# Scores broadcast by transposes, row sums from the accumulator, both deviations in one chain on POOL

## The chip, the core and the metric

The kernel runs on one core of a Trainium2 chip. The time is device time of one execution in microseconds (us). Before the change three runs took 2421.63, 2421.95 and 2422.08 us; the median is 2421.95.

The engines are called as in the profile: PE multiplies matrices (PEld loads its weights), DVE is the vector engine, ACT the scalar engine, POOL the GpSimd engine, and SP issues the DMAs. Each has its own queue of instructions and runs it in order; semaphores tie the queues together.

## The reference

The input x is 128 graphs of 128 nodes with 256 features, adj 128 matrices of 128 x 128. A graph attention layer and a mixture of eight experts follow one another, each behind a layer norm and with a residual:

```python
def _layernorm(x, axis=-1, eps=1e-5):
    m = jnp.mean(x, axis=axis, keepdims=True)
    v = jnp.var(x, axis=axis, keepdims=True)
    return (x - m) / jnp.sqrt(v + eps)

def _L0_gnn_ref(h, adj, W, a):
    Wh = jnp.einsum('bnd,df->bnf', h, W)
    s1 = Wh @ a1
    s2 = Wh @ a2
    e = s1[:, :, None] + s2[:, None, :]
    e = jnp.where(e > 0, e, ALPHA * e)
    e = e + jnp.log(adj + EPS)
    alpha_w = jax.nn.softmax(e, axis=-1)
    return jnp.einsum('bij,bjf->bif', alpha_w, Wh)

def _L0_ffn_ref(x, ...):
    feat = jnp.mean(x, axis=0)
    w = jax.nn.softmax(feat @ Wr + br, axis=-1)
    h = jnp.einsum('bfd,edh->bfeh', x, W1) + b1
    h = jax.nn.relu(_bn(h, g1, be1, m1, v1))
...
    return jnp.einsum('bfed,fe->bfd', y, w)

x = x + _L0_gnn_ref(_layernorm(x, axis=-1), adj, L0_gnn_W, L0_gnn_a)
x = x + _L0_ffn_ref(_layernorm(x, axis=-1), ...)
```

## The kernel before

The 128 graphs are worked in 32 groups of four. The first block (the graph layer, up to about 285 us) takes one group per step in a software pipeline, written out as `step(g, layer)` for each engine. The second block (the experts) takes 32 tiles of eight experts each and is not touched but for a scale factor. The order of work is the order in which each engine's `step` is written; there is no scheduler. Of the 35 steps, seven at the start and four at the end are written out, 24 run in two hardware loops: `layer == 1` (16 steps, which also prepare the first expert weights in two parts, `wq_hi` on ACT and `wq_lo` on POOL) and `layer == 2` (8 steps, `w_hi` and `w_lo`). In step g the group `a` is g - 1, `b` is g - 2, `t` is g - 3, `h` is g - 4 and `nxt` is g + 1.

In one step of the graph layer:

- PE computes h for group b (`ps_h`, from pT and wh, L750), projects group g (`ps_wide`, L734), transposes x of group nxt (`ps_xT`, L703), transposes p of group a (`ps_pT`, L771), and spreads the scores s2 of group g over a square by a product with the identity (`ps_s`, L778). `ps_xT` and `ps_h` are two views of the same memory `ps_th`, in two halves of 512 columns.
- ACT adds s1 (`s_sb`, L508), scales half of x1 for a running sum (`x1s_high`, L516), takes the exponential (`e_sb`, L528), copies a mean (`mean_all`, L534), scales the projection by 1/deviation into `wh` (L548, two pairs of copies), and copies `xnT` (L561) and `pT` (L568) out of PSUM.
- DVE adds the other half to the running sum `acc` (printed as resb, L621), takes the leaky relu (`l_sb`, L636), the reciprocal of the row sums (`rinv`, L640), aggregates the statistics of x1 (`mv`, L594), takes the row maximum (`neg_m`, L645), adds the residual (`x1`, printed as h or w_bc, L664), multiplies by adj (`p_sb`, L674), takes the statistics of the next x (L580) and of x1 (L588), and sums the rows of p (`rowsum`, L686).
- POOL adds `x1s_high` to acc (L441), turns the variance of x1 into `rstd_all` (L449, L452), does its share of the weights (L459 to L476), and turns the statistics of the next x into `rstd` (L403 to L415), the last by a pow.
- SP loads x two groups ahead, stores x1, loads the residual and adj.

Of the kernel before, what the change touches and what calls it, by code (L numbers as in the profile page):

```python
# [24 lines left out]
P = 128  # L25
# [13 lines left out]
def adj_ffn(nc, x, adj, gnn_w, gnn_a, wr, br, w1, b1, g1, be1, m1, v1, w2, b2, g2, be2, m2, v2, wo, bo, out):  # L39
# [17 lines left out]
    with ExitStack() as ctx:  # L57
# [9 lines left out]
        eps_cols = sb("eps_cols", [P, GB])  # L67
# [11 lines left out]
        rstd_all = sb("rstd_all", [P, G, GB])  # L79
# [22 lines left out]
        rstd2_done = sem("rstd2_done")  # L102
# [82 lines left out]
        with ExitStack() as sa:  # L185
# [16 lines left out]
            st1 = [sba(f"st1_{i}", [P, GB, 6]) for i in range(2)]  # L202
            sum1 = sba("sum1", [P, GB])
            dif1 = sba("dif1", [P, GB])
            var1 = sba("var1", [P, GB])
            sqr1 = sba("sqr1", [P, GB])
            ve1 = sba("ve1", [P, GB])
            mean_w = sba("mean_w", [P, P])
            rstd1 = [sba(f"rstd1_{i}", [P, GB]) for i in range(2)]
# [10 lines left out]
            st2 = sba("st2", [P, GB, 6])  # L220
            mv2 = [sba(f"mv2_{i}", [P, GB, 2]) for i in range(2)]
            ve2 = sba("ve2", [P, GB])
# [31 lines left out]
            rstd1_done = sem("rstd1_done", sa)  # L254
# [18 lines left out]
            rowsum_done = sem("rowsum_done", sa)  # L273
# [4 lines left out]
            stats2_done = sem("stats2_done", sa)  # L278
            ve2_done = sem("ve2_done", sa)
# [44 lines left out]
            def _(sp):  # L324
                def load_x(g):
                    p = g[1]
                    wait(sp, xnT_ready, num(g) - 1)
                    wait(sp, bnst1, num(g) - 1)
                    sp.dma_start(x_sb[p][:, :, :], x_g[num(g)]).then_inc(x_loaded[p], 16)
# [13 lines left out]
                def step(g, layer):  # L343
# [24 lines left out]
                    if exists(g):  # L368
                        wait(sp, p_done, num(g) - 1)
                        sp.dma_start(adj_sb[p][:, :, :], adj_g[num(g)]).then_inc(adj_loaded[p], 16)  # L370
# [14 lines left out]
            def _(pool):  # L385
                nc.gpsimd.memset(ident[:, :], 0.0).then_inc(bn_step, 1)
                nc.gpsimd.memset(minus_half[:, :], -0.5).then_inc(w_done, 2)
                nc.gpsimd.memset(eps_cols[:, :], LN_EPS)
# [9 lines left out]
                def rstd_1(g):  # L398

                    p = g[1]  # L400
                    pool.wait_ge(bnst1, num(g) + 1)
                    wait(pool, rstd1_done, num(g))
                    nc.gpsimd.tensor_tensor(dif1[:, :], st1[p][:, :, 1], st1[p][:, :, 4],  # L403
                                            ALU.subtract).then_inc(var1_step, 1)
                    nc.gpsimd.tensor_tensor(sum1[:, :], st1[p][:, :, 2], st1[p][:, :, 5],
                                            ALU.add).then_inc(var1_step, 1)
                    pool.wait_ge(var1_step, 4 * num(g) + 2)
                    nc.gpsimd.tensor_tensor(sqr1[:, :], dif1[:, :], dif1[:, :], ALU.mult).then_inc(var1_step, 1)
                    nc.gpsimd.tensor_scalar(var1[:, :], sum1[:, :], 4.0 / D, 4.0 * LN_EPS, ALU.mult,
                                            ALU.add).then_inc(var1_step, 1)  # L410
                    pool.wait_ge(var1_step, 4 * num(g) + 4)
                    nc.gpsimd.tensor_tensor(ve1[:, :], var1[:, :], sqr1[:, :], ALU.add).then_inc(ve1_done, 1)
                    pool.wait_ge(ve1_done, num(g) + 1)
                    wait(pool, wh_copied, num(g) - 1)
                    nc.gpsimd.tensor_tensor(rstd1[p][:, :], ve1[:, :], minus_half[:, 0:GB],  # L415
                                            ALU.pow).then_inc(rstd1_done, 1)

                def batch_norm_constants():
# [15 lines left out]
                    nc.gpsimd.tensor_tensor(shift, bn_tmp[:, 3], bn_in[:, :, 2, :], ALU.add)  # L434

                def step(g, layer):
                    h = ago(g, 4)
                    if exists(h) and not is_step(h, G - 2) and not is_step(h, G - 1):
                        pool.wait_ge(x1s_high_done, num(h) + 1)
                        wait(pool, acc_high_done, num(h))  # L440
                        nc.gpsimd.tensor_tensor(acc[:, HB:, :], acc[:, HB:, :], x1s_high[:, :, :],  # L441
                                                ALU.add).then_inc(acc_high_done, 1)
                    t = ago(g, 3)
                    if exists(t) and not is_step(t, G - 1):

                        p = t[1]
                        pool.wait_ge(stats2_done, num(t) + 1)
                        wait(pool, rstd2_done, num(t))
                        nc.gpsimd.tensor_tensor(ve2[:, :], mv2[p][:, :, 1], eps_cols[:, :],  # L449
                                                ALU.add).then_inc(ve2_done, 1)  # L450
                        pool.wait_ge(ve2_done, num(t) + 1)
                        nc.gpsimd.tensor_tensor(rstd_all[:, num(t), :], ve2[:, :], minus_half[:, 0:GB],  # L452
                                                ALU.pow).then_inc(rstd2_done, 1)
                        pool.wait_ge(rstd2_done, num(t) + 1)
# [18 lines left out]
                    if layer == 2:  # L473
# [5 lines left out]
                                                ALU.subtract).then_inc(w_done, 1)  # L479
                    nxt = ago(g, -1)  # L480
                    if exists(nxt):
                        rstd_1(nxt)
                    if is_step(g, BN_STEP):
                        batch_norm_constants()
                    if is_step(g, G - 1):
                        tile_sums(pool, 0)
# [4 lines left out]
            def _(act):  # L491
                act.wait_ge(xnT_ready, 1)
# [8 lines left out]
                def step(g, layer):  # L501
# [67 lines left out]
                    if is_step(g, G):  # L569
                        tile_high(act, 0, 2)  # L570
# [710 lines left out]
```

## Time and profile before

| | |
|---|---|
| Median of three runs | 2421.95 us |
| The profiled execution | 2421.09 us |
| Its span on the core | 2419.3 us |
| Mean granted PE clock | 0.993 |
| Busy, whole span | PE 2382.8, DVE 1691.5, ACT 1618.1, POOL 417.0 us |
| pow over 128x4 | 1017 ns in the median of L415 |

The span is the time on the core; 1.8 us lie around it. The busy times add up work over two blocks that are limited differently, so for a change in the graph layer the stage has to be looked at alone. Matmuls overlap each other, so PE counted as busy is not PE at its peak. In the timelines each row is a run of equal instructions: its start, its length, and in brackets how long the engine was idle before it and what ended that.

### The profile page before, as it was taken

The numbers are of one execution on the slowest core, as the hardware profiler recorded it, in microseconds if no ns is written. First come the engines' busy times: TensorE is split into PE (matmuls) and PEld (weight loads), VectorE is DVE, ScalarE is ACT, GpSimd is POOL, SyncE is SP. The second block draws the span as 40 slices with busy tenths as digits, with TensorE's granted clock in tenths as the row PEclk, the third lists the DMA queues.
The fourth block names the chain that finished last, engine by engine and source line by source line (L and its number), as shares of the span: only waits on it lengthen the run. The fifth ranks groups of instructions, "written<-read, shape, count | busy, mean of one in ns | idle before, by whom it ended". The sixth has DMA issues, their size and how long they took to land.

```text
span 2419.3 us, 45995 instructions
## 1 busy us (share of the span) xinstructions
PE 2382.8 (98%) x16292; PEld 2206.4 (91%) x16292; DVE 1691.5 (70%) x2509; ACT 1618.1 (67%) x2524; POOL 417.0 (17%) x553
## 2 busy tenths in 40 slices
PE   8999899999999999999999999999999999999999
PEld 7888689999999999999999999999999999999998
DVE  5999866666666666666666666666666666666666
ACT  5888676666666666666666666666666666666665
POOL 4777521111101011111111101011111111001010
PEclk9999899999999999999999999999999999999999
DMA  5777410000000000000000000000000000000000
GB/s 184 245 239 260 156 36 27 26 26 26 26 26 24 20 9 26 26 26 26 26 26 26 26 26 17 20 14 26 26 26 26 26 26 26 26 26 17 17 10 27
DMA packets 91178, 116.16 MB, mean 48 GB/s; under 512 B 4700, under 2 KB 78856, under 8 KB 91144
## 3 DMA queue, kind: packets, MB, share of 16 engines
q1 hardware_dynamic: 91144, 115.73, 14.4%
q8 instruction: 19, 0.31, 0.1%
q14 instruction: 15, 0.12, 0.0%
HBM read 82.16 MB, written 33.55 MB: 48 GB/s over the span
## 4 chain that ended last, share of the span: by engine, by line
PE 88%; DVE 0%; ACT 0%; issue 0%
PE ps_y L1189 30%; PE ps_wide L171 30%; PE ps_wide L1170 27%; PE ps_t L132 1%; DVE h_lo L1074 0%; DVE z L1067 0%; ACT h_hi L969 0%; ACT v L974 0%; DVE resb L1097 0%; DVE h_lo L1080 0%; DVE z L1057 0%; PE ps_t L1234 0%; PE ps_t L1216 0%; PE ps_t L1221 0%; ACT featT L1000 0%
## 5 line engine op out<-in xcount | busy, mean ns | idle before, releaser
L974 ACT ACTIVATE v<-ps_wide,bn_cols 128x256 f32<-128x256 f32 x768 | 433.9, 565 | 394.9 <-PE ps_wide L1170 258.7
L982 ACT ACTIVATE h<-ps_wide,bn_cols 128x512 f32<-128x512 f32 x512 | 399.0, 779 | 325.4 <-PE ps_wide L171 323.2
L1189 PE MATMUL ps_y<-wo_lo,h_hi 128*128 128x256 f32 x2048 | 578.8, 283 | 0.0
L1189 PE MATMUL ps_y<-wo_hi,h_lo 128*128 128x256 f32 x2048 | 578.3, 282 | 0.0
L1189 PE MATMUL ps_y<-wo_hi,h_hi 128*128 128x256 f32 x2048 | 577.2, 282 | 0.5 <-DVE h_lo L1080 0.5
L1074 DVE SCALAR_TENSOR_TENSOR h_lo<-z,h_hi 128x1024 fp32r<-128x1024 f32 x256 | 313.7, 1225 | 341.7 <-ACT h_hi L969 341.7
L1170 PE MATMUL ps_wide<-xq_hi,wq_hi 128*128 128x256 f32 x1792 | 506.0, 282 | 7.6 <-PEq L185 3.3
L1170 PE MATMUL ps_wide<-xq_lo,wq_hi 128*128 128x256 f32 x1792 | 509.5, 284 | 0.0
L1170 PE MATMUL ps_wide<-xq_hi,wq_lo 128*128 128x256 f32 x1792 | 506.8, 283 | 0.0
L171 PE MATMUL ps_wide<-h_lo,w_hi 128*128 128x512 f32 x1024 | 405.6, 396 | 0.0
L171 PE MATMUL ps_wide<-h_hi,w_lo 128*128 128x512 f32 x1024 | 405.4, 396 | 0.0
L171 PE MATMUL ps_wide<-h_hi,w_hi 128*128 128x512 f32 x1024 | 404.1, 395 | 0.5 <-DVE h_lo L1074 0.5
L1189 PEld LDWEIGHTS ps_y<-wo_hi,h_hi 128*128 128x128 f32 x2048 | 386.5, 189 | 1.1 <-DVE h_lo L1080 0.7
L1189 PEld LDWEIGHTS ps_y<-wo_hi,h_lo 128*128 128x128 f32 x2048 | 387.4, 189 | 0.0
L1189 PEld LDWEIGHTS ps_y<-wo_lo,h_hi 128*128 128x128 f32 x2048 | 386.5, 189 | 0.0
L1080 DVE TENSOR_TENSOR h_lo<-h,h_hi 128x1024 fp32r<-128x1024 f32 x256 | 313.4, 1224 | 95.5 <-ACT h_hi L988 95.5
L1170 PEld LDWEIGHTS ps_wide<-xq_hi,wq_hi 128*128 128x128 f32 x1792 | 340.9, 190 | 20.1 <-issue 4.0
L953 POOL TENSOR_TENSOR resb<-resb,w_bc 128x512 f32<-128x512 f32 x64 | 86.8, 1357 | 1570.5 <-DMA resb<-x_scratch 1563.5
L1170 PEld LDWEIGHTS ps_wide<-xq_hi,wq_lo 128*128 128x128 f32 x1792 | 338.2, 189 | 10.0
L1170 PEld LDWEIGHTS ps_wide<-xq_lo,wq_hi 128*128 128x128 f32 x1792 | 339.8, 190 | 0.0
L1097 DVE SCALAR_TENSOR_TENSOR resb<-ps_y,w_node,resb 128x512 f32<-128x512 f32 x448 | 333.1, 743 | 3.9 <-PE ps_y L1189 3.9
L1067 DVE SCALAR_TENSOR_TENSOR z<-ps_wide,bn_cols,v 128x512 f32<-128x512 f32 x256 | 191.9, 750 | 178.2 <-PE ps_wide L1170 178.2
(132 smaller groups left out, 3002.4 us busy)
## 6 DMA issues: line engine op xcount, KB each, us to landing
x_sb<-in_x SPq DMA_DIRECT2D x32, 512.0 KB, 4.0
res<-in_x SPq DMA_DIRECT2D x32, 512.0 KB, 5.8
x1t<-x_scratch SPq DMA_DIRECT2D x32, 512.0 KB, 3.2
resb<-x_scratch SPq DMA_DIRECT2D x32, 512.0 KB, 3.3
out<-resb SPq DMA_DIRECT2D x32, 512.0 KB, 3.0
adj_sb<-in_adj SPq DMA_DIRECT2D x32, 256.0 KB, 6.1
x_scratch<-h SPq DMA_DIRECT2D x16, 512.0 KB, 4.8
x_scratch<-w_bc SPq DMA_DIRECT2D x16, 512.0 KB, 4.6
```

The lines of the kernel that those rows point to most:

```text
L132: last = nc.tensor.transpose(ps_x[:, c, b4 * N:(b4 + 1) * N], x1t[:, b4, c * P:(c + 1) * P], ident[:, :])
L171: mm = nc.tensor.matmul(acc_ps, w[:, i, c, cols], s[:, c, :], start=start and n == 0, stop=stop and n == len(terms) - 1)
L953: nc.gpsimd.tensor_tensor(resb[:, g, :], resb[:, g, :], ysum[:, g, :], ALU.add).then_inc(resb_done, 1)
L974: nc.scalar.activation(v[:, slot, :], ps_l1[:, 0, 0:H], ACT.Identity, bias=bn_cols[:, 1, cols], scale=bn_cols[:, 0, cols]).then_inc(done, 1)
L982: nc.scalar.activation(h2[:, m, :], ps_l2[:, m, :], ACT.Relu, bias=bn_cols[:, 3, cols], scale=bn_cols[:, 2, cols]).then_inc(r2_done, 1)
L1067: nc.vector.scalar_tensor_tensor(out=z[:, 0, :], in0=ps_l1[:, 1, :], scalar=bn_cols[:, 0, C * e:C * e + 1], in1=v[:, 0:2, :].rearrange("p ...
L1074: nc.vector.scalar_tensor_tensor(out=h1_lo[:, :, :], in0=z[:, :, :], scalar=0.0, in1=h1_hi[:, :, :].bitcast(F32), op0=ALU.max, op1=ALU.sub ...
L1080: nc.vector.tensor_tensor(h2_lo[u[1] % 2][:, :, :], h2[:, :, :], h2_hi[u[1] % 2][:, :, :].bitcast(F32), ALU.subtract).then_inc(lo2_done, 1)
L1097: nc.vector.scalar_tensor_tensor(out=dst[:, g, :], in0=ps_y[:, g, :], scalar=w_node[:, e:e + 1], in1=old, op0=ALU.mult, op1=ALU.add).then_ ...
L1170: mm = nc.tensor.matmul(out_ps, w[:, e, q, :], x[:, q, :], start=start and n == 0, stop=stop and n == len(terms) - 1, skip_group_check=True)
L1189: mm = nc.tensor.matmul(ps_y[:, b4, :], h[:, c, cols], w[:, e, c, :], start=(k == 0 and b4 % per_bank == 0), stop=(k == len(terms) - 1 and ...
```

## The change

The score broadcast on PE becomes four transposes of the broadcast column. PE now transposes p before it transposes the next x, and its waits for `pT` and `xnT` are by halves; ACT copies pT first and then xnT in two halves. p is computed in four quarters, each of which writes its row sum from the accumulator, so the separate row sum goes. The variance of x1 is no longer aggregated on DVE and its mean no longer copied on ACT: POOL computes both deviations (next x and x1) and the means of x1 in one chain, `deviations(k)`, over up to eight columns, into `dev`. `rstd_all` is a view of `dev` and holds half the reciprocal deviation, which a doubled scale in the second block makes good.

```diff
-        rstd_all = sb("rstd_all", [P, G, GB])
+        dev = sb("dev", [P, G + 3, 2 * GB])
+        rstd_all = dev[:, 3:, GB:]
...
+                def deviations(k):
+
+                    p = k[1]
+                    m = ago(k, 3)
+                    cols = slice(0 if exists(k) else GB, 2 * GB if exists(m) else GB)
+                    with_x1 = exists(m)
+                    if exists(k):
+                        pool.wait_ge(bnst1, num(k) + 1)
+                    if with_x1:
+                        pool.wait_ge(bnst2, num(m) + 1)
+                    wait(pool, dev_done, num(k))
+                    nc.gpsimd.tensor_tensor(dif1[:, cols], st[p][:, cols, 1], st[p][:, cols, 4],
                                             ALU.subtract).then_inc(var1_step, 1)
+                    nc.gpsimd.tensor_tensor(sum1[:, cols], st[p][:, cols, 2], st[p][:, cols, 5],
                                             ALU.add).then_inc(var1_step, 1)
...
+                    if with_x1:
+                        nc.gpsimd.tensor_tensor(two_means[:, :], st[p][:, GB:, 1], st[p][:, GB:, 4],
+                                                ALU.add).then_inc(two_means_done, 1)
...
+                        nc.gpsimd.tensor_tensor(mean_all[:, num(m), :], two_means[:, :], half_cols[:, :],
+                                                ALU.mult).then_inc(mean2_done, 1)
...
+                    nc.gpsimd.tensor_tensor(dev[:, num(k), cols], ve1[:, cols], minus_half[:, cols],
+                                            ALU.pow).then_inc(dev_done, 1)
...
@@ ACT, in step
-                        act.wait_ge(rstd1_done, num(g) + 1)
+                        act.wait_ge(dev_done, num(g) + 1)
...
-                    if exists(nxt) and not is_step(nxt, 0):
-                        act.wait_ge(xnT_ready, num(nxt) + 1)
-                        wait(act, wh_ready, 2 * num(nxt))
-                        nc.scalar.activation(xnT[:, :, :], ps_xT, ACT.Copy).then_inc(xnT_copied, 1)
...
                         nc.scalar.activation(pT[:, :, :], ps_pT[:, :, :], ACT.Copy).then_inc(pT_copied, 1)
+                    if exists(nxt) and not is_step(nxt, 0):
+                        wait(act, wh_ready, 2 * num(nxt))
+                        for c in range(C):
+                            act.wait_ge(xnT_ready, C * num(nxt) + c + 1)
+                            nc.scalar.activation(xnT[:, c, :], ps_xT[:, c, :], ACT.Copy).then_inc(xnT_copied, 1)
...
@@ DVE, in step
-                    if exists(t):
-                        aggregate_2(t)
...
-                        nc.vector.scalar_tensor_tensor(out=p_sb[:, :, :], in0=adj_sb[r][:, :, :], scalar=ADJ_EPS,
-                                                       in1=e_sb[:, :, :], op0=ALU.add,
-                                                       op1=ALU.mult).then_inc(p_done, 1)
+                        wait(dve, rinv_done, num(a))
+                        for b4 in range(GB):
+                            last = nc.vector.scalar_tensor_tensor(out=p_sb[:, b4, :], in0=adj_sb[r][:, b4, :],
+                                                                  scalar=ADJ_EPS, in1=e_sb[:, b4, :], op0=ALU.add,
+                                                                  op1=ALU.mult, accum_out=rowsum[:, b4:b4 + 1])
+                            if b4 % HB == HB - 1:
+                                last.then_inc(p_done, 1)
...
-                    if exists(a):
-                        dve.wait_ge(p_done, num(a) + 1)
-                        wait(dve, rinv_done, num(a))
-                        nc.vector.tensor_reduce(rowsum[:, :], p_sb[:, :, :], AX_X, ALU.add).then_inc(rowsum_done, 1)
...
@@ PE, in step
                         for b4 in range(GB):
+                            if b4 % HB == 0 and exists(g):
+                                pe.wait_ge(xnT_copied, C * num(g) + b4 // HB + 1)
                             last = nc.tensor.matmul(ps_h[:, b4, :], pT[:, b4, :], wh[b[1]][:, b4, 0:D], start=True,
                                                     stop=True)
...
+                            if b4 % HB == 0:
+                                pe.wait_ge(p_done, 2 * num(a) + b4 // HB + 1)
...
-                            last = nc.tensor.matmul(ps_s[:, b4, :], wh[g[1]][:, b4, D + 1:D + 2].to_broadcast([P, P]),
-                                                    ident[:, :], start=True, stop=True)
+                            last = nc.tensor.transpose(ps_s[:, b4, :],
+                                                       wh[g[1]][:, b4, D + 1:D + 2].to_broadcast([P, P]), ident[:, :])
```

The order on PE, one step of the first hardware loop, before (ps_th holds h or the transposed x, ps_wide the projection, ps_pT the transposed p, ps_s the scores):

```order
L750 MATMUL ps_th<-wh,pT 128x256 x4
L734 MATMUL ps_wide<-gw,xnT 128x258 x8
L699 ISA
L703 MATMUL ps_th<-ident,x_sb 128x128 x8
L768 REGISTER_ALU
L771 MATMUL ps_pT<-ident,p_sb 128x128 x4
L778 MATMUL ps_s<-ident,wh 128x128 x4
```

The same step after the change:

```order
L733 MATMUL ps_th<-wh,pT 128x256 x2
L732 REGISTER_ALU
L733 MATMUL ps_th<-wh,pT 128x256 x2
L741 ISA
L716 MATMUL ps_wide<-gw,xnT 128x258 x8
L752 ISA
L753 MATMUL ps_pT<-ident,p_sb 128x128 x2
L752 REGISTER_ALU
L753 MATMUL ps_pT<-ident,p_sb 128x128 x2
L681 ISA
L685 MATMUL ps_th<-ident,x_sb 128x128 x8
L762 MATMUL ps_s<-ident,wh 128x128 x4
```

The transposes of p have moved ahead of those of x, and h and p are taken in two halves with a wait ahead of each.

The order on POOL, the odd step of the first hardware loop, before (resb is the running sum, the first ve and rstd_all are those of x1, the rest after wq_lo is the chain of the next x):

```order
L441 TENSOR_TENSOR resb<-resb,x1s_high 128x512
L447 ISA
L449 TENSOR_TENSOR ve<-mv_0,eps_cols 128x4
L452 ISA
L452 TENSOR_TENSOR rstd_all<-ve,minus_half 128x4
L471 ISA
L471 TENSOR_TENSOR wq_lo<-w_stage,wq_hi 128x896
L401 ISA
L403 TENSOR_TENSOR dif<-st_0 128x4
L405 TENSOR_TENSOR sum<-st_0 128x4
```

The same step after the change, as far as the start of its chain:

```order
L463 TENSOR_TENSOR wq_lo<-w_stage,wq_hi 128x896
L474 REGISTER_ALU
L476 TENSOR_TENSOR resb<-resb,x1s_high 128x512
L400 ISA
L402 REGISTER_ALU
L404 TENSOR_TENSOR dif<-st 128x8
L406 TENSOR_TENSOR sum<-st 128x8
L409 TENSOR_TENSOR two_means<-st 128x4
```

The weights' share stands first and the running sum behind it; the separate deviation of x1 is gone from ahead of them, and the chain works on eight columns and has the means in it.

## Rows read from the trace of the kernel before

**Rows 1.** Stages: us, then each engine's busy us (instructions), granted clock, DMA share, GB/s.
```profile
core 0: us, PE busy (x) PEld busy (x) DVE busy (x) ACT busy (x) POOL busy (x), PEclk, DMA share, GB/s
29.21:271.99 242.78, 230.93 (x1320) 203.00 (x1320) 231.81 (x683) 198.06 (x523) 176.62 (x316) 1.00 0.75 242
...
285.70:2419.30 2133.60, 2124.11 (x14849) 1981.54 (x14849) 1439.71 (x1777) 1402.04 (x1959) 223.15 (x200) 1.00 0.07 25
```

**Rows 2.** Timeline of one odd loop step, PE: start us, length us, what.
```profile
101.68 1.99 PE L750 MATMUL ps_th<-wh,pT 128*128 128x256 f32 x8 [0.43 <-ACT pT L568]
...
103.50 3.65 PE L734 MATMUL ps_wide<-gw,xnT 128*128 128x258 f32 x16
...
106.99 1.04 PE L703 MATMUL ps_th<-ident,x_sb 128*128 128x128 f32 x8
...
107.86 0.60 PE L771 MATMUL ps_pT<-ident,p_sb 128*128 128x128 f32 x4
...
108.30 1.06 PE L778 MATMUL ps_s<-ident,wh 128*128 128x128 f32 x8
...
109.79 1.99 PE L750 MATMUL ps_th<-wh,pT 128*128 128x256 f32 x8 [0.43 <-ACT pT L568]
```

**Rows 3.** Timeline of PE in the drain.
```profile
277.29 0.66 PE L771 MATMUL ps_pT<-ident,p_sb 128*128 128x128 f32 x4 [3.30 <-DVE p_sb L674]
278.63 3.78 PE L750 MATMUL ps_th<-wh,pT 128*128 128x256 f32 x8 [0.69 <-ACT pT L568]
```

**Rows 4.** The step of rows 2, ACT.
```profile
107.19 0.84 ACT L548 ACTIVATE wh<-ps_wide,rstd 128x258 f32<-128x258 f32 x2 [0.84 <-PE ps_wide L734]
...
108.14 1.02 ACT L561 ACTIVATE xnT<-ps_th 128x1024 f32<-128x1024 f32 x1
...
109.06 0.59 ACT L568 ACTIVATE pT<-ps_pT 128x512 f32<-128x512 f32 x1
...
109.54 1.14 ACT L508 ACTIVATE s_sb<-ps_s,wh 128x128 f32<-128x128 f32 x4
```

**Rows 5.** The step of rows 2, DVE.
```profile
102.61 0.69 DVE L636 SCALAR_TENSOR_TENSOR l_sb<-s_sb 128x512 f32<-128x512 f32 x1 [0.34 <-ACT s_sb L508]
103.22 0.17 DVE L640 RECIPROCAL rinv<-rowsum 128x4 f32<-128x4 f32 x1
...
103.31 0.35 DVE L594 BATCH_NORM_AGGREGATE mv<-st 128x2 f32<-128x6 f32 x4
...
103.57 0.65 DVE L645 TENSOR_REDUCE neg_m<-l_sb 128x4 f32<-128x512 f32 x1
...
105.71 0.68 DVE L674 SCALAR_TENSOR_TENSOR p_sb<-adj_sb,e_sb 128x512 f32<-128x512 f32 x1
...
106.31 1.40 DVE L580 BATCH_NORM_STATS2 st<-x_sb 128x6 f32<-128x256 f32 x4
...
107.95 0.67 DVE L686 TENSOR_REDUCE rowsum<-p_sb 128x4 f32<-128x512 f32 x1
...
108.53 1.07 DVE L588 BATCH_NORM_STATS2 st<-w_bc 128x6 f32<-128x256 f32 x3
...
109.52 0.86 DVE L621 SCALAR_TENSOR_TENSOR resb<-h,rstd_all,resb 128x256 f32<-128x256 f32 x2
```

**Rows 6.** The step of rows 2, POOL.
```profile
106.28 2.10 POOL L471 TENSOR_TENSOR wq_lo<-w_stage,wq_hi 128x896 f32 x1 [0.20 <-POOL rstd_all L452]
...
108.34 0.20 POOL L403 TENSOR_TENSOR dif<-st 128x4 f32<-128x4 f32 x1
...
109.69 1.16 POOL L415 TENSOR_TENSOR rstd<-ve,minus_half 128x4 f32<-128x4 f32 x1 [0.16 <-POOL ve L412]
...
111.55 1.27 POOL L441 TENSOR_TENSOR resb<-resb,x1s_high 128x512 f32<-128x512 f32 x1 [0.70 <-ACT x1s_high L516]
```

**Rows 7.** Groups by line, POOL, 0 to 300: busy us, mean ns | idle before.
```profile
L428 POOL TENSOR_TENSOR bn_tmp<-bn_tmp,minus_half 128x32 f32<-128x32 f32 x1 | 5.4, 5449 | 0.1
```

**Rows 8.** Timeline of the drain, at 281.1.
```profile
280.02 2.30 POOL L441 TENSOR_TENSOR resb<-resb,x1s_high 128x512 f32<-128x512 f32 x1 [1.64 <-issue]
...
281.13 1.48 DVE L621 SCALAR_TENSOR_TENSOR resb<-w_bc,rstd_all,resb 128x256 f32<-128x256 f32 x1
```

More of the change, by code:

```diff
@@ L326, in load_x @@
                     p = g[1]
-                    wait(sp, xnT_ready, num(g) - 1)
+                    wait(sp, xnT_ready, 2 * (num(g) - 1))
                     wait(sp, bnst1, num(g) - 1)
@@ L434, in batch_norm_constants @@
                     nc.gpsimd.tensor_tensor(shift, bn_tmp[:, 3], bn_in[:, :, 2, :], ALU.add)
+                    nc.gpsimd.tensor_tensor(bn_cols[:, 0, :], bn_cols[:, 0, :], bn_cols[:, 0, :], ALU.add)
                 def step(g, layer):
[L437 to L454, printed above, removed]
                     if layer == 1 and g[1] == 0:
@@ L585, in stats_2 @@
                     if b4 == 0:
-                        wait(dve, stats2_done, num(g))
+                        wait(dve, dev_done, num(g) + 2)
                         dve.wait_ge(x1_done, num(g) + 1)
-                    part = nc.vector.bn_stats(st2[:, b4, :], x1[g[1]][:, b4, :])
+                    part = nc.vector.bn_stats(st[1 - g[1]][:, GB + b4, :], x1[g[1]][:, b4, :])
                     if b4 == GB - 1:
                         part.then_inc(bnst2, 1)
-                def aggregate_2(g):
-                    for b4 in range(GB):
-                        last = nc.vector.bn_aggr(mv2[g[1]][:, b4, :], st2[:, b4, :])
-                    last.then_inc(stats2_done, 1)
                 dve.wait_ge(col_mean_ready, 1)
@@ L764, in step @@
                         tile_transpose(pe, 0, ps_x0)
+                    if exists(a):
+                        wait(pe, pT_copied, num(a))
+                        for b4 in range(GB):
+                            if b4 % HB == 0:
+                                pe.wait_ge(p_done, 2 * num(a) + b4 // HB + 1)
+                            last = nc.tensor.transpose(ps_pT[:, b4, :], p_sb[:, b4, :], ident[:, :])
+                        last.then_inc(pT_ready, 1)
                     if exists(nxt) and not is_step(nxt, 0):
                         next_rows(nxt)
-                    if exists(a):
-                        pe.wait_ge(p_done, num(a) + 1)
-                        wait(pe, pT_copied, num(a))
-                        for b4 in range(GB):
-                            last = nc.tensor.transpose(ps_pT[:, b4, :], p_sb[:, b4, :], ident[:, :])
-                        last.then_inc(pT_ready, 1)
                     if exists(g):
```

109 lines of the change are left out of this document (47 added, 62 removed).

## The prediction

> **What bounds the kernel now.** I read first the table of stages, then one step of the first stage engine by engine. Times within a step are counted from the start of its h product on PE; "effective" is the distance from one instruction's start to the next one's, about 0.1 us less than its duration, because neighbours overlap.
>
> The first stage runs from 29.21 to 271.99 in 30 steps, 242.78 us, or 8.09 a step; the experts' stage takes 2133.6 us with PE busy for 2124 of them [rows 1]. The change leaves the instructions of that second stage as they are (one scale factor, and one POOL instruction with an operation more ahead of it), so I book nothing there. What can move is those steps, the two before them and the drain.
>
> In the step at 101.68, PE runs h for 1.82 (101.68 to 103.50), the projection for 3.49 (to 106.99), the transposes of x for 0.87, those of p for 0.44 and the score broadcast until 109.36, and then idles 0.43 until 109.79, 8.11 after the step began [rows 2]. What it waits for is on ACT: the second pair of wh copies cannot start before the projection's end (107.19, or 5.51 into the step); behind it stand the xnT copy, ending 109.16, and the pT copy, ending 109.65. PE follows 0.14 later [rows 4]. DVE is nearly full too: of its 8.11 us turn it idles only the 0.34 before l_sb [rows 5]. So PE, ACT's chain and DVE are all within half a microsecond of the bound; the change must relieve all three.
>
> **The change part by part.**
>
> PE, broadcast by transposes. Four broadcasts ran as 8 passes in 1.06 us; four transposes of p of the same size ran as 4 passes in 0.60 [rows 2]. I take the new ones at the latter: -0.46. PE's own work falls from 8.11 - 0.43 = 7.68 to 7.22.
>
> ACT, p first and xnT in halves. From 5.51: the wh pair takes 0.75 effective, plus about 0.06 because its scale is now addressed by a register computed in the loop; then pT 0.48 effective (109.06 to 109.54), then the first half of xnT, which is 512 columns like pT, 0.59; then the 0.14 handoff [rows 4]. h starts at 5.51 + 0.81 + 0.48 + 0.59 + 0.14 = 7.53 instead of 8.11. The second half of xnT ends 0.48 later, long before h's second pair of products needs its bank. The transposes of p must be ready by 6.3, which needs the last quarter of p by about 5.9. s_sb now follows the second xnT half, at about 7.75. Its broadcasts on PE stand behind the x transposes, ready at about 7.3: not late.
>
> DVE. Gone are the four aggregations, 0.26 effective (103.31 to 103.57), and the row sum, 0.58 (107.95 to 108.53); the p product, 0.60 (105.71 to 106.31), becomes four quarters with a sum each. Without aggregations neg_m waits some 0.05 more for l_sb. The turn is 8.11 - 0.34 - 0.26 - 0.58 - 0.60 + 0.05 = 6.38 plus the four quarters [rows 5]. No row has this operation. From below: splitting and summing are free, 4 x 0.15 = 0.60. From above: each quarter costs as much as a 256-element one (0.86 for two) and a small instruction of 0.17 behind it without overlap, 4 x 0.60 = 2.4. I take 0.30 each: 0.15 for the elements, 0.06 fixed, 0.09 for reading out the sum, as the reciprocal's distance 103.22 to 103.31; together 1.2, the value nearer to the small-instruction rows because everything else on this engine overlaps. Turn: 7.58.
>
> The Trainium skill ("VectorE: DVE Perf Modes", Two Vector instructions with no wait between them) says that an operation that writes its accumulator out is two instructions. That is why a second small one is in my estimate; no row of this kernel shows it.
>
> POOL. Six short operations and two pow (4 columns each) become one chain over 8 columns, with two more for the means, and the pow grows: 4 columns took 1.16, 32 took 5.45, so 0.153 a column and 1.77 for 8 [rows 6, 7]. From the first operation to the pow's start it was 1.35 (108.34 to 109.69); with two more queued instructions of about 0.15 it is 1.65. The chain takes 3.4. It used to begin once x's statistics were there, in the middle of DVE's turn; it now begins after the statistics of x1 as well, which are DVE's last work of the step. And ACT's wh copies of the next step wait for it. The ACT copy of the means, 0.19, goes, into slack.
>
> So the new time is this. DVE in a 7.58 turn starts l_sb at 1.4, x1 at 2.7, p at 4.3, and ends the x1 statistics at 8.2. Undisturbed, the chain is through at 11.7, 4.1 into the next step; the first wh pair must be on its way by 4.7 to be out of the way at 5.51. That holds with 0.6 to spare. But it meets DVE's acc additions and l_sb, 1.4 us of instructions with two SBUF operands each. At 280.02 POOL's addition took 2.30 instead of 1.27, and DVE's single addition 1.48 instead of some 0.45 [rows 6, 8]: such pairs run one after the other. The chain's short dependent operations must slip between or wait until l_sb is done, which I price at 1.0 (1.3 is left of acc and l_sb when the chain begins, 0.3 of it is used). wh is then ready at 12.7, second pair at 13.45 instead of 13.1; as the loop DVE statistics, chain, wh, s_sb, l_sb, statistics spans two steps, half of these 0.36 falls on each: 7.75 a step.
>
> The Trainium skill ("SBUF — State Buffer", Who interferes with whom) calls the port pair that VectorE and GpSimd share an exclusive lock, held for the whole instruction, whenever VectorE reads two SBUF operands and GpSimd reads SBUF. The trace agrees (the 1.48). It speaks against this change, since it moves seven POOL reads onto the additions; without it the step would be 7.58.
>
> In the 16 steps that prepare the first expert weights POOL has a further 2.10 (wq_lo) and 1.27 (acc) in every odd step [rows 6], behind the chain now: 3.4 + 1.0 + 2.1 + 1.27, and some 0.3 in which it waits for p's quarters, is 8.07. The even steps have four short sums instead of about the same length. I take 8.0 for these 16. Their acc addition then ends as the next statistics do. wq_lo ends about 0.7 deeper in the step than now (108.38, 6.7 in), and SP, which waits for it before it issues the weights and behind them the loads of x, residual and adj, moves with it; these are needed a step or more later, so I book nothing.
>
> Sum, in the profiled execution (2421.09: span 2419.3 and 1.8 around it): 16 x 0.11 = 1.8; 14 other steps x 0.36 = 5.0, less 0.6 as the early ones without loop registers are shorter already; 1.2 for the broadcasts and one aggregation in the start-up and drain, where the split p and the chain give some of it back. Together 7.4: 2413.7. The median of the runs is 0.86 above the profiled one: 2414.5.
>
> **Rivals.**
>
> The coupling through POOL costs nothing (short reads slip in between). For it: the pow at 109.69, issued during an addition, took 1.16, only 0.15 over the usual. Against it: the 1.48. Every step 7.58: 30 x 0.51 = 15.3, plus 1.2 less 0.6: 2421.95 - 15.9 = 2406.1, and 2404.5 if the quarters are cheaper too and ACT's 7.53 decides.
>
> The summed quarters cost 0.44 each, because the read-out waits for the quarter's end. DVE's turn is 8.14, the old step, and only the 1.2 is left, within the noise: 2421. For it: short operations rarely overlap fully; against it: 0.09 for the reciprocal.
>
> The other side: the quarters alone make it slower. Place: DVE between x1 and the x statistics. At the upper price of 2.4 the turn is 8.78, 0.69 over the old step, 30 times, 21 less 1.2: 2442. It decides from 1.73 for the four (parity) and makes the kernel measurably slower from 1.93. DVE has no idle time left to cover it.
>
> The clock. The stage ran at granted 1.00, the 2.4 GHz level [rows 1]; after waits of 3.3 and 0.7 us in the drain h took 3.78 instead of 1.99, which is the 1.2 GHz level [rows 2, 3]. If PE's higher share of transposes let it fall for good, PE's 7.22 would double, 6.3 us more a step, some 2600 in all. Against it: 1.3 us of transposes in a row in every step of rows 2 and no fall, and idle time shrinks.
>
> The Trainium skill ("TensorE: Matmul & The Clock Gate", Part 4: PE-mode transpose) says that transposes do not count as PE activity for the clock. By it this rival gains; every step now has 1.9 us of them without a break. The trace so far gives it little.
>
> **Chances.** Forecast 0.45 (own range 2409 to 2418), free coupling 0.25, quarters at parity 0.20, quarters clearly dear 0.05, clock 0.03, else 0.02. From 2403 to 2422 the first three are covered. A difference under 0.2% (4.8 us) can't be told from none, so faster means below 2417.1: 0.40 of the forecast, all of the free coupling, 0.05 of the parity case: 0.70. Slower 0.08, the same 0.22.
>
> **What would show it.** Broadcast group near 0.6 a step; h starting about 0.14 after the first xnT half; p quarters from 4.3 to 5.5; steps of about 7.75, and 8.0 in the 16 weight steps. If wh copies are released by POOL's dev rather than by the projection, the coupling is real. If DVE has no idle time before l_sb, the quarters set the turn. The prediction is wrong if the steps are equal in all stretches, or if the granted clock leaves 1.00 between 30 and 255 us.

## The result

The changed kernel takes 2380.39 us in the median (2378.61 to 2381.81) against 2421.79; the ratio is 0.9827, 95% interval 0.9816 to 0.9839. The forecast was 2414.5 with a range down to 2403: the direction was right, the size was not. The profiled execution has a span of 2379.0 us, 40.3 less than before.

The windows of the changed kernel, PE alone, cut as in [rows 1], with the last one ending at the last experts' product:

```profile
core 0: us, PE busy (x), PEclk, DMA share, GB/s
29.62:267.14 237.52, 222.06 (x1200) 1.00 0.77 249
267.14:280.34 13.20, 6.55 (x21) 0.71 0.17 68
280.34:2374.60 2094.26, 2088.97 (x14848) 1.00 0.07 25
```

The 30 steps took 242.78 and take 237.52: 5.3 less. From their end to the first experts' product it was 13.75 (271.99 to 285.74) and is 13.20. The experts' products themselves, from the first to the last, took 2129.1 us (285.74 to 2414.85) and take 2094.3: **34.8 of the 40.3 us lie in a stage whose products the change does not touch.**

PE there is busy all the time, in both. Only the number of products that fit into the same 600 us differs (before, then after):

```profile
600.00:1200.00 600.00, 600.00 (x4213) 1.00 0.07 24
```

```profile
600.00:1200.00 600.00, 600.00 (x4286) 1.00 0.07 24
```

That is 142.4 against 140.0 ns a product, at the same granted clock of 1.00, the 2.4 GHz level; times 14848 products it is 36 us. Single starts show which ones. A product takes two operands from SBUF, the core's memory: `xq` and `wq` in the first layer, `h1` and `w` in the second, `h2` and `wo` in the third, each in a high and a low part (`_hi`, `_lo`; `h1` and `h2` are printed as h). The rows are start and length, before and after, and show every third product, the one of the two high parts.

```profile
1000.77 0.28 PE L1170 MATMUL ps_wide<-xq_hi,wq_hi 128*128 128x256 f32 x1
...
1001.13 0.28 PE L1170 MATMUL ps_wide<-xq_hi,wq_hi 128*128 128x256 f32 x1
...
1001.84 0.28 PE L1189 MATMUL ps_y<-wo_hi,h_hi 128*128 128x256 f32 x1
...
1002.20 0.28 PE L1189 MATMUL ps_y<-wo_hi,h_hi 128*128 128x256 f32 x1
```

```profile
1000.37 0.28 PE L1155 MATMUL ps_wide<-xq_hi,wq_hi 128*128 128x256 f32 x1
...
1000.71 0.28 PE L1155 MATMUL ps_wide<-xq_hi,wq_hi 128*128 128x256 f32 x1
...
1001.05 0.28 PE L1174 MATMUL ps_y<-wo_hi,h_hi 128*128 128x256 f32 x1
...
1001.41 0.28 PE L1174 MATMUL ps_y<-wo_hi,h_hi 128*128 128x256 f32 x1
```

From one row to the next it is three products: 0.36 us before and 0.34 after in the first layer, 0.36 in both in the third. The distance from one start to the next, at each place of a tile, has these medians over 30 tiles. For `xq` they are 116 to 127 ns before and 113 after (118 at one place in ten; in both kernels one place of some 200 is left out); for the 512-column second layer 228 to 235 and 226 to 232. For `wo` they are 117 to 124 before, and 120 at most places after.

A step of the graph stage after, the one with `wq_lo`, PE, ACT, DVE and POOL, in the loop with the first expert weights (compare [rows 2, 4 to 6]):

```profile
99.01 0.60 PE L762 MATMUL ps_s<-ident,wh 128*128 128x128 f32 x4
99.48 1.99 PE L733 MATMUL ps_th<-wh,pT 128*128 128x256 f32 x8
...
100.86 1.03 POOL L406 TENSOR_TENSOR sum<-st 128x8 f32<-128x8 f32 x1
...
103.11 1.65 POOL L424 TENSOR_TENSOR dev<-ve,minus_half 128x8 f32 x1 [0.19 <-POOL ve L420]
104.02 0.28 DVE L658 SCALAR_TENSOR_TENSOR p_sb<-adj_sb,e_sb 128x128 f32<-128x128 f32 x1
104.23 0.09 DVE L658 DVE_READ_ACCUMULATOR p_sb<-adj_sb,e_sb 128x1 f32 x1
...
104.65 0.29 DVE L658 SCALAR_TENSOR_TENSOR p_sb<-adj_sb,e_sb 128x128 f32<-128x128 f32 x1
104.73 2.16 POOL L463 TENSOR_TENSOR wq_lo<-w_stage,wq_hi 128x896 f32 x1
...
104.90 1.58 ACT L541 ACTIVATE wh<-ps_wide,dev 128x258 f32<-128x258 f32 x4 [1.04 <-POOL dev L424]
...
106.82 1.11 ACT L562 ACTIVATE xnT<-ps_th 128x512 f32<-128x512 f32 x2
...
107.50 0.70 PE L733 MATMUL ps_th<-wh,pT 128*128 128x256 f32 x2 [0.33 <-ACT xnT L562]
```

The quarters of p are 0.21 apart. POOL's short sum takes 1.03 where DVE's additions and `l_sb` run beside it (0.43 in the steps between; 0.20 in g2, below, at 111.39 with no such instruction of DVE beside it), and `wh` is released by POOL's `dev`, as forecast. And `wq_lo` starts 0.08 us after the last quarter has started: the experiments show what hangs on that. From h to h the 16 steps alternate 7.59 and 8.02, 7.80 in the mean.

In the loop with the second weights the last quarter is just too late:

```profile
214.13 1.29 POOL L468 TENSOR_TENSOR w_lo<-w_stage,w_hi 128x512 f32 x1 [0.70 <-ACT w_hi L532]
214.22 0.08 DVE L658 DVE_READ_ACCUMULATOR p_sb<-adj_sb,e_sb 128x1 f32 x1
214.22 1.35 DVE L658 SCALAR_TENSOR_TENSOR p_sb<-adj_sb,e_sb 128x128 f32<-128x128 f32 x1
...
215.63 0.44 PE L753 MATMUL ps_pT<-ident,p_sb 128*128 128x128 f32 x2 [0.74 <-DVE p_sb L658]
```

It takes 1.35 instead of 0.28, and PE waits 0.74. In the steps between these the quarters are through in time and `wh` waits for POOL's `dev` instead:

```profile
222.72 1.58 ACT L541 ACTIVATE wh<-ps_wide,dev 128x258 f32<-128x258 f32 x4 [0.50 <-POOL dev L424]
```

So six of the eight steps stay at 8.06 to 8.08 (the first is 7.49, the last 8.15).

### The profile page after: what moved, and what is told of

Read it like the earlier page. It is cut to its first block, busy times and chain, and to the rows that moved or that the text cites. A ratio compares the mean times of both kernels' runs of the same rounds, so it can differ in the third digit from the quotient of the medians.

```text
span 2379.0 us, 46022 instructions
## 1 busy us (share of the span) xinstructions
PE 2339.6 (98%) x16164; PEld 2166.8 (91%) x16164; DVE 1687.8 (71%) x2577; ACT 1615.7 (68%) x2524; POOL 435.0 (18%) x566
## 4 chain that ended last, share of the span: by engine, by line
PE 88%; DVE 0%; ACT 0%; issue 0%
PE ps_y L1174 31%; PE ps_wide L171 30%; PE ps_wide L1155 26%; PE ps_t L132 1%; DVE h_lo L1059 0%; DVE z L1052 0%; ACT h_hi L954 0%; ACT v L959 0%; DVE resb L1082 0%; DVE h_lo L1065 0%; DVE z L1042 0%; PE ps_t L1219 0%; PE ps_t L1201 0%; PE ps_t L1206 0%; ACT featT L985 0%
## 5 line engine op out<-in xcount | busy, mean ns | idle before, releaser
L1155 PE MATMUL ps_wide<-xq_hi,wq_hi 128*128 128x256 f32 x1792 | 500.9, 279 | 7.4 <-PEq L185 3.1
L1155 PE MATMUL ps_wide<-xq_lo,wq_hi 128*128 128x256 f32 x1792 | 497.8, 278 | 0.0
L1155 PE MATMUL ps_wide<-xq_hi,wq_lo 128*128 128x256 f32 x1792 | 497.0, 277 | 0.0
L171 PE MATMUL ps_wide<-h_hi,w_hi 128*128 128x512 f32 x1024 | 398.3, 389 | 0.5 <-DVE h_lo L1059 0.5
L1174 PEld LDWEIGHTS ps_y<-wo_hi,h_lo 128*128 128x128 f32 x2048 | 392.5, 192 | 0.0
```

The lines of the kernel that those rows point to most:

```text
L171: mm = nc.tensor.matmul(acc_ps, w[:, i, c, cols], s[:, c, :], start=start and n == 0, stop=stop and n == len(terms) - 1)
L1155: mm = nc.tensor.matmul(out_ps, w[:, e, q, :], x[:, q, :], start=start and n == 0, stop=stop and n == len(terms) - 1, skip_group_check=True)
L1174: mm = nc.tensor.matmul(ps_y[:, b4, :], h[:, c, cols], w[:, e, c, :], start=(k == 0 and b4 % per_bank == 0), stop=(k == len(terms) - 1 and ...
```

## Experiments: where the operands stand

"Distance" below is the place of `xq` less that of `wq` in a partition, in bytes, mod 256 (the same for `h1` and `w`), from the order and sizes in which the kernels declare their tensors; "stage" is from the first experts' product to the last. `h2` and `wo` move with `xq`, and their own distance stays 0 but where it is said.

**e1, e2, e3: before, with padding of 608, 32 or 64 bytes.** The edit of e1 (32 and 64 bytes are `[P, 8]` and `[P, 16]`):

```diff
-        rstd_all = sb("rstd_all", [P, G, GB])
+        rstd_all = sb("rstd_all", [P, G, GB]); pad = sb("pad", [P, 152])
```

> The kernel before with 608 unused bytes a partition behind rstd_all, the amount by which dev is larger than rstd_all: xq, h1, h2 and wo lie in SBUF where they lie after the change, and no instruction is changed. Placement theory (the expert stage gained 36 us because its operands moved from 32 to 0 modulo 64 bytes): 2421.8 - 36 = 2386, matmul starts of the x_q products 0.114 us apart instead of 0.1185. Rival (the gain comes from the changed instructions: another program length, the clock after another drain, the operation in the start-up): 2421.8, no change.

> The kernel before with 32 unused bytes in the same place. If what counts is the address modulo 64: 2386 as with 608. If it counts modulo 128 or more (the change moved the operands by 608, to 0 modulo 128 for h1 and xq): only a part of it or nothing, 2400 to 2422.

> The kernel before with 64 unused bytes there: operands moved, but still 32 modulo 64. Modulo-64 theory: no change, 2421.8. If any shift that changes the distance to the weights helps (larger units): below 2415.

Measured: 2387.95 (ratio 0.9858, 0.9842 to 0.9874), 2419.19 (0.9987, 0.9976 to 0.9997) and 2413.93 (0.9963, 0.9948 to 0.9979). Not one instruction of e1 differs from before, and it has 34 of the 41 us. So the place of the tensors is the cause, and not the changed instructions, the length of the program or the drain (the last four steps) ahead of the stage. e2 puts `xq` at a multiple of 64 bytes, where the changed kernel has it too, and gains 3 us: the place mod 64 doesn't decide. The row of e1:

```profile
600.00:1200.00 600.00, 600.00 (x4284) 1.00 0.07 24
```

**e4: the changed kernel, 32 bytes further.**

```diff
+        rstd_all = dev[:, 3:, GB:]; pad = sb("pad", [P, 8])
```

> The changed kernel with 32 unused bytes behind dev: its expert operands are back at 32 modulo 64. Placement theory: it loses the 36 us of the expert stage and keeps the 5 of the graph stage: 2380.4 + 36 = 2416. Rival (changed instructions): stays at 2380.

2421.47 (0.9998, 0.9988 to 1.0007): the whole gain is gone, though the graph stage ends as early as after (first experts' product at 279.68). It is 5 us more than was expected, as this distance, 96, makes the stage 6.5 us longer than the 224 of before (the table below).

```profile
600.00:1200.00 600.00, 600.00 (x4200) 1.00 0.07 24
```

**e5, f1, h2: only the third layer's operands moved.** e5 puts 64 bytes in front of `wo_hi`, h2 128 bytes, f1 64 in front of `h2_hi` and 64 in front of `wo_hi`.

```diff
+            padw = sbb("padw", [P, 16]); wo_hi = sbb("wo_hi", [P, E, C, D], F32R)
```

> The changed kernel with 64 bytes per partition put in front of wo_hi, so that wo_hi and wo_lo of the experts' third layer stand 64 bytes (mod 128) from h2, with which they are multiplied, instead of 0; nothing else moves. The theory that the issue rate of a matmul hangs on the distance of its two operands mod 128 expects the third layer's products (192 in each of 32 tile passes, 6144 in all) to go from a mean of about 120.0 ns to 113.5 to 115 ns from start to start: 31 to 40 us less, 2341 to 2350 us. The theory that only the absolute place of the moving operand counts expects nothing or a loss from 0 to 64, 2380 to 2400 us.

> The changed kernel with 64 bytes in front of h2_hi and 64 more in front of wo_hi: h2 stands at 64 mod 128, wo stays at 0, so that all three layers' products have the same alignment (moving operand at 0, stationary operand at 64 mod 128), which only layers 1 and 2 have in the changed kernel. Theory 1, PE falls into one rhythm as long as all operand pairs are aligned alike: the third layer's products join the 113 ns of the first's, 6144 x 6 ns = 35 us less, 2340 to 2350 us. Theory 2, no simple rule (e5 has shown that moving wo alone slows the xq products, which it doesn't touch): anything between 2370 and 2425 us. Theory 3, layer 3 is slow for another reason than its alignment (it has two alternating stationary operands whatever their place): 2378 to 2383 us.

> The changed kernel with 128 bytes in front of wo_hi: the third layer's operands are 128 mod 256 apart instead of 0 and nothing else moves. In e5 (64 apart) its products went from 120.0 to 117.5 ns, and those of layer 1, which do not move, from 113.5 to 117.5: the stage took 2108.2 instead of 2094.3 us. If the products' rhythm is carried over from layer to layer, any other place of wo disturbs layers 1 and 2: 2385 to 2420 us. If wo at 128 keeps layer 1 at 113.5 ns and brings layer 3 to 113.5 to 117.5 ns: 15 to 37 us less, 2343 to 2366 us.

2391.49, 2392.04 and 2393.49 us (0.9875, 0.9871, 0.9885). All three are 11 to 13 us slower than the changed kernel, and every theory that promised a gain fell; what held were the wide ranges without one (e5's second theory, by absolute place, falls with e6 below). In e5 the products of `wo` fell from 120 to about 117.5 ns, but those of `xq`, whose places hadn't moved, rose from 113 to about 118. The spacing of a layer's products thus hangs on the place of another layer's operands too; that it is carried over from product to product is a guess that no run tests.

**e6, f2, g3, g4, h1: the distance by itself.** e6 (before) shifts `wq` and `w` by 64 and the rest by 160 bytes; the others are the changed kernel with 128, 512, 256 and 64 bytes behind `dev`.

> The kernel before, with 64 bytes in front of wq_hi and 96 more behind rstd_all: the quarter weights wq and the weights w stand at 0 mod 128 instead of 64, xq and h1 at 64 instead of 32. The distance of the two operands of the xq products is 64 as in the changed kernel, but both places are exchanged. The distance theory expects the xq products at 113 to 115 ns and the whole within 5 us of e1 (2388); the theory that the moving operand has to stand at 0 mod 128 expects them at 117 ns or more, and 2405 to 2425 us.

> The changed kernel with 128 bytes behind the deviations: every place mod 128 as in the changed kernel, mod 256 and above not. If only places mod 128 count, the pattern of the intervals is the changed kernel's to the ns, and the time 2379 to 2382 us. If the layout counts in larger units (256, 512 bytes) or everything is a matter of exact places, 2390 to 2425 us.

> The changed kernel with 512 bytes behind the deviations. If the distance between the two groups of operands (wq, w, below the deviations, and xq, h1, h2, wo, above) counts mod 512, as a single weight row of 128 fp32 columns has 512 bytes: the changed kernel's intervals to the ns, a tile pass of 65.0 us and 2379 to 2382 us. If it counts mod 1024 or in exact places: another pattern, a pass of 65.3 to 66.3 us and 2390 to 2425 us.

> The same with 256 bytes. If the distance counts mod 256: 65.0 us for a tile pass and 2379 to 2382 us, as in the changed kernel; if mod 512 only: another pattern, 65.3 to 66.3 us and 2390 to 2425 us.

> The changed kernel with 64 bytes behind the deviations: the distance of xq, h1 from wq, w becomes 128 mod 256. The five slow distances lie on both sides (96: 2135.6 us for the experts' stage, 192: 2125.2), so if 64 is a single fast place, as the rows so far have it: 2122 to 2136 us for the stage and 2408 to 2422 us for the whole. If 128, half the period, is fast too (operands half a period apart never meet): 2094 us or less, and 2375 to 2381 us.

2388.15, 2409.95, 2379.56, 2379.82 and 2415.45 us. With the others:

| distance mod 256 | kernels | stage, us |
|---|---|---|
| 0 | e2 | 2126.0 |
| 32 | e3 | 2122.2 |
| 64 | after, e1, e6, f3, f4, g1, g2, g3, g4 | 2093.8 to 2095.6 |
| 96 | e4 | 2135.6 |
| 128 | h1 | 2129.4 |
| 192 | f2 | 2125.2 |
| 224 | before, e7, e8 | 2129.1 to 2129.3 |

What counts is the distance between the two groups, not the place of either: e6 and h1 have `xq`, `h1`, `h2` and `wo` at the same place mod 256 and differ by 35 us in the stage, and the slow kernels have `wq` and `w` where the changed kernel has them. The distance counts mod 256 (f2 against g3, g4). Of the seven distances tried one is fast. With it, putting `wo`, or `h2` and `wo`, elsewhere, 64 or 128 bytes apart instead of 0, costs 11 to 14 us of the stage (2108.2, 2105.6, 2107.1). Why the fast distance is 64, which of the layers needs it, and how one layer's operands slow another's products, stays open.

## Experiments: the parts of the change in the graph stage

**e7, e8, f3: one part alone, on before.** e7 has the transposes for the broadcast, e8 the quarters with `pT` ahead of `xnT`, f3 the joint chain on POOL, each as in the diff above. **f4** is the changed kernel without the transposes:

```diff
-                            last = nc.tensor.transpose(ps_s[:, b4, :],
-                                                       wh[g[1]][:, b4, D + 1:D + 2].to_broadcast([P, P]), ident[:, :])
+                            last = nc.tensor.matmul(ps_s[:, b4, :], wh[g[1]][:, b4, D + 1:D + 2].to_broadcast([P, P]),
+                                                    ident[:, :], start=True, stop=True)
```

> The kernel before with one part of the change: the broadcast of the scores (ps_s) by four transposes instead of four fp32 matmuls; no tensor moves. My step chains give 0.46 us less on PE in each step, all of it on the step's path only if PE's chain carries it: 30 steps x 0.2 to 0.46 would be 6 to 14 us, but by the chain of the step (ACT and DVE between two PE parts) a part is eaten by POOL's release of wh and by the whole p. Theory 1 (the transposes shorten the loop by themselves): the first experts' matmul starts 3 to 6 us earlier than before's 285.74. Theory 2 (they only pay together with the earlier deviations): under 1.5 us earlier. Experts' stage unchanged at 2133.6 us within 1.5.

> The kernel before with another part alone: p written in four accumulating quarters (no separate row sum on DVE), its transposes in front of those of x, xnT copied in halves behind pT. No tensor moves. Prediction's terms: the quarters cost 4 x 0.21 to 0.30 us against 1.09 and give 0.7 us of DVE back by the dropped row sum. Theory 1: it brings 1 to 3 us over the stage (first experts' matmul at 282.7 to 284.7). Theory 2 (the earlier pT is eaten by the later xnT): within 0.7 us of 285.74.

> Of the change only the third part: both deviations and the means formed jointly on POOL, none on DVE and ACT; the broadcast by fp32 matmuls, the whole p with its separate row sum and the old order of the transposes stay. Tensors stand where the changed kernel has them, so the experts' stage should take the changed kernel's time (2374.6 - 280.3 = 2094.3 us to the last matmul, within 1.5). Graph stage: theory 1 (this part carries the gain; DVE loses 4 aggregates and wh is released earlier): first experts' matmul at 280 to 283 us. Theory 2 (no part brings anything alone, only together): 285 to 290 us.

> The changed kernel with the broadcast of the scores back as fp32 matmuls, everything else as changed. Before with the transposes alone gained 0.7 us in the graph stage (e7). If the gain of the transposes hangs on the other parts, this kernel loses more than 0.7: the prediction's 0.46 us per step on the path would be 14 us, of which at most the stage's 5.4 can be lost, 283 to 287 us for the first experts' matmul. If it is a part by itself: 280.5 to 281.5 us.

| kernel | us | first experts' product | from the first step's start to it | loop steps with first weights | with second |
|---|---|---|---|---|---|
| before | 2421.8 | 285.74 | 256.5 | 8.11 | 8.11 |
| e7 transposes | 2421.38 | 285.06 | 256.5 | 8.11 | 8.11 |
| e8 quarters | 2426.04 | 289.60 | 260.6 | 7.92 / 9.37 | 7.6 / 7.68 |
| f3 POOL chain | 2389.30 | 286.83 | 257.6 | 8.11 (one 9.01) | 8.11 |
| f4 all but transposes | 2417.01 | 317.71 | 288.0 | 8.53 / 11.91 | 7.47 / 8.40 |
| after | 2380.39 | 280.34 | 250.7 | 7.59 / 8.02 | 8.06 / 8.08 |

(f3 and f4 have the fast distance.) The first of the 30 steps starts at 29.06 to 30.73 us in before, e1, e2, e3 and e6, whose instructions are the same, so the time from there compares better than the third column. By it no part gains alone: they bring 0.0, -4.1 and -1.1 us, together 5.8, and all but the transposes lose 31.5. e7 and f3 came out as their second theories had it; e8 and f4 as none had. The parts don't add up; one clash decides. In e8, DVE, POOL and PE:

```profile
106.98 2.07 POOL L471 TENSOR_TENSOR wq_lo<-w_stage,wq_hi 128x896 f32 x1 [0.20 <-POOL rstd_all L452]
107.04 0.08 DVE L677 DVE_READ_ACCUMULATOR p_sb<-adj_sb,e_sb 128x1 f32 x1
107.04 2.16 DVE L677 SCALAR_TENSOR_TENSOR p_sb<-adj_sb,e_sb 128x128 f32<-128x128 f32 x1
```

```profile
109.26 0.44 PE L772 MATMUL ps_pT<-ident,p_sb 128*128 128x128 f32 x2 [1.73 <-DVE p_sb L677]
```

`wq_lo` starts 0.06 us ahead of the fourth quarter instead of 0.08 behind it, and the quarter takes 2.16. In f4 it is the third that is caught, and the fourth by the addition behind it:

```profile
135.27 2.08 POOL L463 TENSOR_TENSOR wq_lo<-w_stage,wq_hi 128x896 f32 x1
135.31 2.18 DVE L658 SCALAR_TENSOR_TENSOR p_sb<-adj_sb,e_sb 128x128 f32<-128x128 f32 x1
...
137.31 1.31 POOL L476 TENSOR_TENSOR resb<-resb,x1s_high 128x512 f32<-128x512 f32 x1
...
137.43 1.34 DVE L658 SCALAR_TENSOR_TENSOR p_sb<-adj_sb,e_sb 128x128 f32<-128x128 f32 x1
...
138.83 0.69 PE L753 MATMUL ps_pT<-ident,p_sb 128*128 128x128 f32 x2 [2.62 <-DVE p_sb L658]
```

After such waits PE also got a lower clock, 0.91 from 140 to 190 us, and the eight transposes of x behind the wait of 2.62 took 1.91 where those of the step before took 1.04:

```profile
128.84 1.04 PE L685 MATMUL ps_th<-ident,x_sb 128*128 128x128 f32 x8
...
139.31 1.91 PE L685 MATMUL ps_th<-ident,x_sb 128*128 128x128 f32 x8
```

```profile
140.00:190.00 50.00, 42.70 (x218) 0.91 0.60 196
```

In e8, where PE idles 1.73 in such a step, the granted clock stays at 1.00 over the same 50 us.

**g1, g2: POOL's two long sums in pieces**, on f4 and on the changed kernel.

```diff
-                        nc.gpsimd.tensor_tensor(wq_lo[:, e, :, :], w_stage[:, 0:Q, :],
-                                                wq_hi[:, e, :, :].bitcast(F32), ALU.subtract).then_inc(wq_done, 1)
+                        for i in range(Q):
+                            last = nc.gpsimd.tensor_tensor(wq_lo[:, e, i, :], w_stage[:, i, :],
+                                                           wq_hi[:, e, i, :].bitcast(F32), ALU.subtract)
+                        last.then_inc(wq_done, 1)
```

> f4 (the changed kernel with the broadcast as fp32 matmuls), with POOL's two long sums in pieces: wq_lo (2.08 us) as 7 sums of 128 columns, the addition to acc (1.31 us) as 4. In f4's trace two of DVE's four p quarters took 2.18 and 1.34 us instead of 0.28, each beside one of these sums, and the weight steps alternate 8.53 and 11.91 us. Theory 1, DVE can't start a two-operand instruction while a POOL sum holds the port they share: a quarter waits for one piece at most (about 0.4 us), the pair of weight steps goes from 20.4 to 16 to 17 us, and the first experts' matmul from 317.7 to 282 to 292 us. Theory 2, the loss of f4 is the TensorE clock (0.91 to 0.94 in these steps) and the fp32 broadcast itself: the pair of steps stays above 19 us and the stage above 310 us.

> The changed kernel with POOL's two long sums in pieces as in g1. Its steps alternate 7.59 and 8.02 us, the drain step 9.29 has a p quarter of 1.14 us behind an addition to acc. Theory 1 (the port): the drain step loses about 1 us and the odd weight steps up to 0.3 us each; against it 9 more POOL instructions in two steps cost POOL 0.1 us each. First experts' matmul 277 to 280 us, total 2377 to 2380 us. Theory 2: POOL's chain is the longer one (wh waits for the deviations) and the pieces delay it: 281 to 284, 2381 to 2384 us. The experts' stage keeps its places.

g1: 2387.04 us, first experts' product at 286.55, 31 us earlier than f4; the steps are 7.97 and 8.37. In the steps with the first weights no quarter takes over 0.56:

```profile
106.09 3.03 POOL L464 TENSOR_TENSOR wq_lo<-w_stage,wq_hi 128x128 f32 x7
106.14 0.08 DVE L662 DVE_READ_ACCUMULATOR p_sb<-adj_sb,e_sb 128x1 f32 x1
106.14 0.56 DVE L662 SCALAR_TENSOR_TENSOR p_sb<-adj_sb,e_sb 128x128 f32<-128x128 f32 x1
...
109.09 2.05 POOL L480 TENSOR_TENSOR resb<-resb,x1s_high 128x128 f32<-128x128 f32 x4
```

In the loop with the second weights, where `w_lo` was left whole, a quarter still takes 1.35 in every second step, as in f4. So the cause of f4's loss is that DVE's quarters stand behind POOL's long sums. The broadcast by fp32 matmuls is the same in g1, and the granted clock there is 1.00 from 100 to 190 us: the lower clock of f4 came with the waits, and what part of its loss is the clock's stays open. The Trainium skill ("SBUF — State Buffer", Who interferes with whom) names a port pair that the two engines share as a lock held for a whole instruction; the traces agree, with 2.16 us for a quarter of 0.28. g2: 2389.11 us, 9 slower than the changed kernel, the other theory's direction and beyond its 2384: where the clash was avoided anyway, the pieces only lengthen POOL's work (`wq_lo` 3.02 for 2.17, the addition 2.07 in the mean for 1.27), and ACT's next `x1s_high` waits for it, 10.1 us in all from 60 to 190 where it waits for nothing in the changed kernel:

```profile
L518 ACT ACTIVATE x1s_high<-h,dev 128x256 f32<-128x256 f32 x16 | 7.3, 510 | 10.1 <-POOL resb L480 10.1
```

The steps go to 7.92 and 8.72. No kernel tried beats the changed one by more than its spread.

## Why the prediction was wrong

**The step that failed** is "so I book nothing there", on the experts' stage. Its instructions were indeed the same; their operands' places were not, and 34.8 us hung on that (e1, e4). A look at the change of declared sizes, 512 to 1120 bytes, would have shown that something moves; no row of the trace before gave its price. The prediction's own signs of being wrong looked at the graph stage alone, and neither came: the steps differ between the stretches, and the granted clock is 1.00 there.

**The sum for the graph stage**, 7.4 us, came out at 5.4 (first experts' product at 280.34 for 285.74; 5.8 from the first step's start). It is near by luck, with errors of both signs in it:

- The 16 steps with the first weights: forecast 8.0, measured 7.80; 4.9 us gained where 1.8 were booked. POOL's wait for p's quarters that was priced at 0.3 doesn't occur, and the last quarter escapes `wq_lo` by 0.08 us, which is luck; the steps without `wq_lo` run at 7.59.
- The other 14: 4.4 us booked (5.0 less 0.6), 0.4 measured. In the loop with the second weights 7.75 was forecast and 8.07 measured, because in every second step the last quarter meets `w_lo` there (1.35 us), and in the others `wh` waits for `dev`. The coupling was looked for between the POOL chain and DVE's additions, and it is there: the chain takes 4.0 to 4.2 in the loops where 3.4 and 1.0 were booked. The dearer one, DVE's quarters behind POOL's long sums, was not in the sum; it had only POOL's 0.3 for the quarters, in one stretch. One step takes 9.29: DVE also normalises the first tile in it (1.38), and its first quarter takes 1.14 beside the addition on POOL.
- The quarters: 1.2 us for the four forecast, 0.85 measured (104.02 to 104.87, 0.21 each); the read-out is a small instruction of 0.08. The Trainium skill ("VectorE: DVE Perf Modes", Two Vector instructions with no wait between them) has it as a second instruction; the trace agrees. The rival of dear quarters had the price of a quarter wrong, yet e8 shows that the quarters without the other parts do make the graph stage slower (4.1 us), by another mechanism.
- Broadcast 0.60 to 0.65 (forecast 0.60), pow over 8 columns 1.65 (forecast 1.77), no fall of the clock (1.00 in the steps): right. But the 0.46 that the broadcast saves on PE is worth nothing alone (e7) and 37 us of this stage with the rest (f4).

## What to carry to other kernels

Before a stage is booked as unchanged, compare the places of its operands, not only its instructions: where PE is the bound, a padding between the groups of operands, in steps of 32 bytes up to 224, is a cheap experiment (of seven distances one was fast here), and a measured gain of 1 to 2% from any edit that resizes a buffer should be tested against the old kernel with the same padding. And look in every step for DVE instructions with two SBUF operands that start within a few hundredths of a microsecond of a long POOL instruction (0.08 ahead of it a quarter took 0.29 here, 0.06 behind it 2.16): parts that shift by that much don't add up.

## What the runs showed of the hardware

- Back-to-back products of the experts' operands (type fp32r) of 256 columns start 112 to 127 ns apart and those of 512 columns 226 to 239 (medians at each place of a tile), at the same granted clock; the stage takes 2094 to 2136 us by the distance in bytes of its operand tensors mod 256, and nine kernels with distance 64 agree within 1.8 us. The Trainium skill ("SBUF — State Buffer", Who interferes with whom) names the port pair of VectorE and GpSimd as the only contention, with two independent read ports for PE. It says nothing there of where an operand stands, and the runs here show that this counts.
- A POOL sum of 128 x 896 takes 2.08 us in one piece (f4) and 3.03 in seven (g1). A DVE quarter of 0.28 that starts behind it takes 2.16 to 2.18 (e8, f4), and at most 0.56 behind a piece (g1).
